# Banded attention chunks that hold a wide and a narrow head together, with a fourth query and key stack

## The chip, the cores and the metric

The kernel runs on one core of a Trainium2 chip. The metric is device time in microseconds (us) of one execution; several executions are timed and their median is given, and one more is profiled.

## The reference

One transformer layer, post-norm, on x of shape [2, 2048, 256]: attention with 16 heads of 16 columns and ALiBi bias, a residual and a layer norm, then a routed mixture of 7 experts with a no-op expert, a residual and a layer norm. The part that matters here is the attention:

```python
n_heads = 16; head_dim = 16
qkv = (x @ Wqkv + bqkv).reshape(B, L, 3, n_heads, head_dim)
scores = einsum('bqhd,bkhd->bhqk', q, k) / sqrt(head_dim)
scores = scores + slopes[None, :, None, None] * (-|i - j|)
probs = softmax(scores, axis=-1)
out = einsum('bhqk,bkhd->bqhd', probs, v).reshape(B, L, D)
x = layernorm(x + out @ Wout + bout)
```

The slope of head h is 2^(-h/2). Where slope times distance is beyond 104 the probability is zero, so head h needs only a band around the diagonal: 104 positions to each side for head 0, 1177 (rounded up to 16) for head 7, nearly everything from head 8 on.

## The kernel before, in words

The kernel has four stages on all engines: projections (to 113 us of the profiled execution), attention (to 785 us), output projection and routing, experts. Only attention is touched.

An **item** is one head of one batch: 32 of them. `ITEMS` lists them in pairs, a wide head (8 to 15) and then the narrow head with a number lower by 8. An item has 16 key blocks of 128 keys, and each key block has a **span** of query columns, the band around it (`spans`). `packed` lays the spans of all items one behind another into **chunks** of 1536 columns (three PSUM banks of 512): `CHAIN`, 489 chunks. A chunk holds pieces (item, key block, first and last query column, column in the chunk). As the items follow each other whole, a run of some 21 chunks of a wide head is followed by 5 to 20 chunks of the narrow one. In a wide chunk a piece is up to 1536 columns long, in a chunk of head 0 it is at most 336.

For each chunk c, in this order on the engines:

- **Scores**, TensorE, `score(c)`, the matmul of L987: for each piece, `score_cuts` splits the columns where the diagonal block begins or ends and at bank borders; each cut is 4 weight loads and 4 bf16 matmuls, one for each group of 32 array columns (32 keys each). They go to banks 0 to 2 or 3 to 5 by the parity of c. `score(c)` waits for the exponential of chunk c - 2 (`expd`), and in an item's first chunk for its loaded stack (`stack_in`).
- **Exponential**, ScalarE, one ACTIVATE of the whole chunk, L1031, from the banks into `prob`, a ring of 8 chunks in SBUF.
- **Diagonal blocks**, L1045: each key block's own 128 columns are multiplied with a table, even key blocks on VectorE and odd ones on GpSimd (heads 2 and 3 twice).
- **Values**, TensorE, `pv(c)`, L1011: `value_runs` splits each piece by query block j; block j goes to the column group j % 4, so each group keeps its own part of the output in PSUM bank 6 + n % 2. `value_turns` lines the runs of the four groups up in turns, the group with the most columns last. Each turn is one f32 matmul, two weight loads and two matmuls in the trace. `pv(c - 4)` stands behind `score(c)` on TensorE (`VALUE_LAG = 4`, `value_bursts`).
- **Division**, VectorE, in the slots of `divide_plan`: six slots after an item's last chunk the sums are copied out of PSUM (TAKE, L1053), and in one slot each follow SPREAD (L1059), four INVERT (a reciprocal of 128 columns, L1064) and SCALE (L1070). A slot also holds the diagonal blocks of the chunk of that number.

GpSimd copies an item's values into `v_head` (L1098) at the item's first chunk. SyncE's queue, in the order of the items, loads each item's query and key rows into one of three **stacks** (`STACKS = 3`, 11 DMAs of L259 to L293; item 0 is loaded earlier from ScalarE's queue), waiting for the last scores of the item three before, and stores the output of the item three before (L937).

## Time and profile before

| | |
|---|---|
| median of 3 runs | 1063.8 us (1063.44 to 1067.05) |
| profiled execution | 1064.59 us |
| its span, first to last instruction | 1062.8 us |
| TensorE busy | 1015.1 us, 96% |
| ScalarE busy | 811.9 us, 76% |
| VectorE busy | 453.5 us, 43% |
| GpSimd busy | 321.1 us, 30% |
| mean granted TensorE clock | 0.981 of 2.4 GHz |

The profiled execution lies 0.8 us above the median of the runs, and 1.8 us of it are outside the span. A busy share of TensorE is not its load at full rate: matmuls overlap, and their ends are modelled.

### The profile page before, as it was taken

The page shows a single profiled execution, that of the slowest core. Times are in us where ns is not written, and L with a number is a line of the kernel's source. Part 1 is how long each engine was busy: PE and PEld are TensorE (multiplying, and loading weights), DVE is VectorE, ACT ScalarE, POOL GpSimd, SP SyncE. Part 2 cuts the span into 40 slices and gives each one's busy share as a digit, 9 for nine tenths or more (in the row PEclk, how much of TensorE's full clock was granted, in tenths as well). Part 3 has the DMA queues.
Part 4 walks back from the last instruction along what each step waited for, and adds up shares of the span by engine and source line. Part 5 has one row for each costly group of instructions (what it writes and reads, how often), then busy time and mean ns, then how long its engine had stood idle before and what let it go on. Part 6 is the DMA issues. An engine that isn't in the chain of part 4 may idle for free. (4 is left out here: it accounts for less than half of the span.)

```text
span 1062.8 us, 40378 instructions
## 1 busy us (share of the span) xinstructions
PE 1015.1 (96%) x17922; PEld 720.6 (68%) x17922; DVE 453.5 (43%) x1064; ACT 811.9 (76%) x807; POOL 321.1 (30%) x486
## 2 busy tenths in 40 slices
PE   9999899999999999999999999999997399999997
PEld 6555576776676776877666776868686256666665
DVE  5778324564352432325355624323257611111165
ACT  3564799999999999999999999999966164211152
POOL 3333122234121121112232721211330255555433
PEclk9999999999999999999999999999999599999999
DMA  6755312212222111112332221120209246544473
GB/s 195 222 189 173 110 57 72 58 59 83 53 67 61 51 46 46 47 45 68 103 109 64 53 82 54 49 65 25 87 12 301 48 135 174 125 116 113 114 282 133
DMA packets 76562, 104.87 MB, mean 99 GB/s; under 512 B 13774, under 2 KB 62556, under 8 KB 76380
## 3 DMA queue, kind: packets, MB, share of 16 engines
q1 hardware_dynamic: 65852, 87.94, 26.6%
q0 software_dynamic: 6080, 9.06, 4.1%
q10 hardware_dynamic: 4448, 5.19, 1.5%
q8 instruction: 144, 2.36, 0.9%
q14 instruction: 38, 0.31, 0.1%
HBM read 66.49 MB, written 31.48 MB: 92 GB/s over the span
## 5 line engine op out<-in xcount | busy, mean ns | idle before, releaser
L1031 ACT ACTIVATE prob<-ps 128x1536 f32<-128x1536 f32 (+5 forms) x489 | 660.6, 1533 | 13.4 <-PE ps L987 12.1
L987 PE MATMUL ps<-q_stack,k_stack 111*32 111x512 bf16 (+25 forms) x9308 | 467.3, 302 | 7.0 <-issue 5.1
L1011 PE MATMUL ps<-prob,v_head 128*32 128x128 f32 (+6 forms) x7288 | 467.6, 338 | 2.5 <-issue 2.5
L987 PEld LDWEIGHTS ps<-q_stack,k_stack 111*32 111x32 bf16 (+2 forms) x9308 | 257.2, 96 | 132.2 <-ACT prob L1031 70.5
L1011 PEld LDWEIGHTS ps<-prob,v_head 128*32 128x32 f32 x7288 | 291.0, 110 | 53.4 <-issue 4.9
L1045 POOL TENSOR_TENSOR prob<-prob,near_bias 128x128 f32<-128x128 f32 x288 | 141.7, 496 | 500.6 <-ACT prob L1031 497.5
L1045 DVE TENSOR_TENSOR prob<-prob,near_bias 128x128 f32<-128x128 f32 x288 | 97.9, 348 | 400.4 <-ACT prob L1031 399.2
L1064 DVE RECIPROCAL o_rec<-o_den 128x128 f32<-128x128 f32 x128 | 113.8, 924 | 0.7
L1744 PE MATMUL ps<-xeT,w 128*128 128x512 f32 x224 | 99.2, 601 | 0.8 <-ACT xeT L1775 0.7
L1821 ACT ACTIVATE hT<-ps 128x512 f32<-128x512 f32 x28 | 16.7, 596 | 106.5 <-PE ps L1744 106.5
L1758 PE MATMUL ps<-w,hT 128*128 128x256 f32 x448 | 97.9, 379 | 0.0
L1758 PEld LDWEIGHTS ps<-w,hT 128*128 128x128 f32 x448 | 84.8, 190 | 11.5 <-issue 0.5
L1744 PEld LDWEIGHTS ps<-xeT,w 128*128 128x128 f32 x224 | 43.1, 193 | 52.9 <-issue 50.6
L502 PE MATMUL ps<-xT,w_qkv 128*128 128x512 f32 x128 | 60.1, 599 | 1.0 <-DVE w_qkv L740 1.0
L615 ACT ACTIVATE split<-ps,bias_qk_columns 128x512 bf16<-128x512 f32 x32 | 22.0, 687 | 44.3 <-PE ps L502 42.0
L1979 DVE TENSOR_SCALAR hT<-ps 128x512 f32<-128x512 f32 x28 | 19.4, 692 | 79.7 <-PE ps L1744 79.7
L863 POOL TENSOR_TENSOR square<-split 128x512 bf16<-128x512 bf16 x32 | 33.6, 1050 | 64.0 <-ACT split L615 63.9
L2032 POOL DMA_INDIRECT token_sums<-ye,slot_token x20 | 31.6, 1578 | 60.4 <-DVE ye L1995 42.3
L2012 POOL DMA_INDIRECT xe<-z_rows,slot_token x28 | 28.4, 1013 | 52.6 <-DVE slot_token L1582 44.4
L502 PEld LDWEIGHTS ps<-xT,w_qkv 128*128 128x128 f32 x128 | 23.6, 190 | 23.1 <-issue 19.4
L1995 DVE TENSOR_SCALAR ye<-ps,slot_weights 128x256 f32<-128x256 f32 x20 | 9.7, 484 | 65.5 <-PE ps L1758 65.5
L511 PEld LDWEIGHTS ps<-w_qkv,xT 128*128 128x128 f32 x128 | 24.1, 190 | 14.6 <-issue 10.5
(175 smaller groups left out, 610.7 us busy)
## 6 DMA issues: line engine op xcount, KB each, us to landing
qk_parts<-split SPq DMA_DIRECT2D x32, 384.0 KB, 3.0
w<-L_ffn_experts_inter_dram SPq DMA_DIRECT2D x7, 1024.0 KB, 6.4
w<-n_L_ffn_experts_out_dram SPq DMA_DIRECT2D x7, 1024.0 KB, 9.5
q_stack<-qk_parts SPq DMA_DIRECT2D x31, 192.0 KB
k_stack<-qk_parts SPq DMA_DIRECT2D x31, 192.0 KB
z_rows<-v SPq DMA_DIRECT2D x8, 516.0 KB, 8.8
heads<-o_out SPq DMA_DIRECT2D x128, 32.0 KB, 2.4
v<-in_L_attn_x_dram SPq DMA_DIRECT2D x8, 512.0 KB, 6.8
```

Source lines behind the costliest of these rows:

```text
L502: mm = pe.matmul(ps[:, 2 + m, :], w[:, k, m * P:(m + 1) * P], xT[n % 2][:, k, :], start=(k == 0), stop=(k == 1))
L511: mm = pe.matmul(ps[:, 6 + s % 2, 0:DX], xT[n % 2][:, k, s * P:(s + 1) * P], w[:, k, 2 * D:3 * D + EXTRA], start=(k == 0), stop=(k == 1))
L863: pool.tensor_tensor(square[m][:, :], split[m][:, 0, :], split[m][:, 0, :], ALU.mult)\
L987: mm = pe.matmul(ps[k:k + 32, SLOT_BANKS * (c % 2) + bank, col:col + z - a], k_st[n % STACKS][0:rows, kb * P + k:kb * P + k + 32], q_st[n ...
L1011: mm = pe.matmul(ps[32 * g:32 * g + 32, 6 + n % 2, column:column + width * times], vh[n % 2][:, kb, :], moving, start=(n, g) not in begun, ...
L1031: act.activation(prob[:, c % RING, 0:at + z - a], ps[:, bank:bank + SLOT_BANKS, :].rearrange("p c n -> p (c n)")[:, 0:at + z - a], ACT.Exp ...
L1045: eng.tensor_tensor(here, here, near[:, h, :], ALU.mult).then_inc(done, 1)
L1064: dve.reciprocal(o_rec[:, mine], o_den[:, mine]).then_inc(o_step, 1)
L1744: mm = pe.matmul(ps[:, 2 + j % 2, :], w1[par][:, k, j * P:(j + 1) * P], xeT[par][:, k, :], start=(k == 0), stop=(k == 1))
L1758: mm = pe.matmul(ps[:, 4 + s, 0:D], hT[:, j, s * P:(s + 1) * P], w2[par][:, j, :], start=(j == 0), stop=(j == FT - 1))
L2012: pool.indirect_dma_start(out=xe[e % 2][:, s, :], out_offset=None, in_=z_rows, in_offset=bass.IndirectOffsetOnAxis(ap=t["slot_token"][:, e ...
L2032: pool.indirect_dma_start(out=acc_rows, out_offset=bass.IndirectOffsetOnAxis(ap=t["slot_token"][:, e, s:s + 1], axis=0), in_=ye[e % 2][:, ...
```

## The change

- `packed` and `fill` give way to `mixed`: a pair of items (wide, narrow) is laid out together. The first 4 chunks of a pair hold the wide head alone; from then on each chunk begins with a share of the narrow head's columns (every second chunk a quarter more than the share) and is filled up with the wide head's. The share is sized so that the narrow head ends at least 3 chunks ahead of the wide one. Each pair begins a new chunk, so its last chunk may be short. `CHAIN` has 494 chunks.
- An item's chunks now overlap those of its partner, and the narrow item ends first. `ENDING` and `RANK` order the items by their last chunk for the division and the stores. `place_of` gives each item its output bank and values buffer, and `place_user_before` the item that must have ended before.
- There are four stacks. The fourth lies in the SBUF of `split`, a tile of the projections; item 3's load now waits for the stores from it (`parts_out`). Stores still follow the load of the item three on (`STORE_LAG = 3`).
- `part_shift` and `widen_shift` of the second batch (8 small VectorE instructions) move from the start of attention to slots 6, 7 and 8.
- `BIAS_AT` of the second batch goes by the chunk count. In the general branch, which these inputs don't take, a semaphore is replaced by others.

```diff
-STACKS = 3
+STACKS = 4
+STORE_LAG = 3
+NARROW_FROM, WIDE_LAST = 4, 3
+SHIFT_SLOT = 6
...
+def next_pieces(left, at, room):
+    pieces = []
+    while left and room > 0:
+        n, kb, a, end = left[0]
+        z = min(end, a + room)
+        if kb * P < z < kb * P + P:
+            z = kb * P
+        if z <= a:
+            break
+        pieces.append((n, kb, a, z, at))
+        at, room = at + z - a, room - (z - a)
+        left[0] = (n, kb, z, end)
+        if z == end:
+            left.pop(0)
+    return pieces, at
+
+def mixed(wide, narrow):
+    (n, h), (m, g) = wide, narrow
+    left = [[(item, kb, a, z) for kb, a, z in spans(head, 0)] for item, head in (wide, narrow)]
+    columns = [sum(z - a for *_, a, z in mine) for mine in left]
+    shared = -(-(sum(columns) - (NARROW_FROM + WIDE_LAST) * WIDTH) // WIDTH)
+    share = -(-columns[1] // shared // 16) * 16
+    chunks = []
+    while left[0] or left[1]:
+        pieces, at = [], 0
+        if len(chunks) >= NARROW_FROM and left[1]:
+            pieces, at = next_pieces(left[1], at, min(share + share // 4, WIDTH) if len(chunks) % 2 else share)
+        more, at = next_pieces(left[0], at, WIDTH - at)
+        if not left[0] and not more:
+            more, at = next_pieces(left[1], at, WIDTH - at)
+        chunks.append(pieces + more)
+    return chunks
...
-CHAIN = packed(ITEMS)
+CHAIN = [chunk for n in range(0, len(ITEMS), 2) for chunk in mixed((n, ITEMS[n][1]), (n + 1, ITEMS[n + 1][1]))]
...
+ENDING = sorted(range(len(ITEMS)), key=lambda n: LAST[n])
+RANK = [ENDING.index(n) for n in range(len(ITEMS))]
+
+def place_of(n):
+    return (n // 2 + n % 2) % 2
+
+def place_user_before(n):
+    earlier = [m for m in range(len(ITEMS)) if place_of(m) == place_of(n) and LAST[m] < FIRST[n]]
+    return max(earlier, key=lambda m: LAST[m]) if earlier else None
...
         if slot - VALUE_LAG - 2 in LAST:
-            n = LAST.index(slot - VALUE_LAG - 2)
+            n = RANK[LAST.index(slot - VALUE_LAG - 2)]
...
             if (b, h) == ITEMS[H]:
                 sp.wait_ge(t["shift_out"], 32)
+            if n == STACKS - 1:
                 for m in range(4):
                     sp.wait_ge(t["parts_out"][m], 16 * NCH)
...
-            if n >= STACKS:
-                store_turned_heads(n - STACKS)
+            if n >= STORE_LAG:
+                store_turned_heads(n - STORE_LAG)
...
-                    if n >= 2:
-                        pe.wait_ge(o_read, n - 1)
+                    if place_user_before(n) is not None:
+                        pe.wait_ge(o_read, RANK[place_user_before(n)] + 1)
...
-                mm = pe.matmul(ps[32 * g:32 * g + 32, 6 + n % 2, column:column + width * times],
-                               vh[n % 2][:, kb, :], moving, start=(n, g) not in begun, stop=False,
+                mm = pe.matmul(ps[32 * g:32 * g + 32, 6 + place_of(n), column:column + width * times],
+                               vh[place_of(n)][:, kb, :], moving, start=(n, g) not in begun, stop=False,
...
-        part_shift(dve, t, 1, 4)
-        for part in range(3):
-            widen_shift(dve, t, 1, part)
         for slot, steps in enumerate(DIVIDE):
+            if slot == SHIFT_SLOT:
+                part_shift(dve, t, 1, 4)
+            if 0 <= slot - SHIFT_SLOT < 3:
+                widen_shift(dve, t, 1, slot - SHIFT_SLOT)
...
+            split = v_life.enter_context(nc.sbuf_tensor("split", [P, 4, 3, CH], BF16))
+            t["split"] = [split[:, m, :, :] for m in range(4)]
+            spare = split[0:ROWS, :, :, :].rearrange("p m c n -> p (m c n)")
+            t["q_stack"].append(spare[:, 0:L])
+            t["k_stack"].append(spare[:, L:2 * L])
```

## Rows read from the trace of the kernel before

**Rows 1.** Costliest groups: busy, mean ns of one, then idle before and its releaser.

```profile
L1031 ACT ACTIVATE prob<-ps 128x1536 f32<-128x1536 f32 (+5 forms) x489 | 660.6, 1533 | 13.4 <-PE ps L987 12.1
...
L1011 PE MATMUL ps<-prob,v_head 128*32 128x128 f32 (+6 forms) x7288 | 467.6, 338 | 2.5 <-issue 2.5
```

**Rows 2.** Waits: total us, times, longest; the first three of attention.

```profile
PEld ps L987 <- ACT prob L1031: 70.5, 174, 1.4
...
PEld ps L987 <- issue: 14.5, 34, 1.7
...
ACT prob L1031 <- PE ps L987: 12.1, 16, 2.9
```

**Rows 3.** Timeline, ScalarE: start, us, calls, idle before; attention's exponentials.

```profile
114.17 5.48 ACT L1031 ACTIVATE prob<-ps 128x1536 f32<-128x1536 f32 x4 [2.89 <-PE ps L987]
119.88 1.45 ACT L1031 ACTIVATE prob<-ps 128x1536 f32<-128x1536 f32 x1 [0.23 <-PE ps L987]
122.16 23.09 ACT L1031 ACTIVATE prob<-ps 128x1536 f32<-128x1536 f32 x17 [0.82 <-PE ps L987]
...
785.29 1.28 ACT L1445 ACT_TABLE_LOAD   x1
```

**Rows 4.** Timeline, ScalarE, short windows: one wide stretch, then heads 4, 5 and 6.

```profile
405.05 20.28 ACT L1031 ACTIVATE prob<-ps 128x1536 f32<-128x1536 f32 x15
...
294.49 15.95 ACT L1031 ACTIVATE prob<-ps 128x1536 f32<-128x1536 f32 x11
...
336.96 8.74 ACT L1031 ACTIVATE prob<-ps 128x1536 f32<-128x1536 f32 x6
...
383.18 11.14 ACT L1031 ACTIVATE prob<-ps 128x1536 f32<-128x1536 f32 x8
```

**Rows 5.** Windows, busy us and instructions of each engine: one wide, then around heads 1 and 4.

```profile
282.00:293.00 11.00, 11.00 (x272) 6.92 (x268) 1.17 (x4) 11.00 (x9) 2.39 (x5) 1.00 0.17 45
...
176.30:194.20 17.90, 17.39 (x618) 14.76 (x610) 6.78 (x16) 17.14 (x14) 6.19 (x13) 1.00 0.24 79
...
296.20:307.60 11.40, 11.40 (x378) 10.98 (x372) 6.70 (x14) 11.18 (x8) 3.54 (x7) 1.00 0.12 45
```

**Rows 6.** Instruction queue (packets, MB, share), then TensorE's timeline in head 0's chunks.

```profile
q8 instruction: 144, 2.36, 0.9%
...
145.16 0.44 PE L987 MATMUL ps<-q_stack,k_stack 123*32 123x80 bf16 x21 [0.41 <-issue]
...
149.04 0.26 PE L987 MATMUL ps<-q_stack,k_stack 111*32 111x112 bf16 x4 [1.04 <-issue]
```

**Rows 7.** Start of attention: timeline of SyncE's queue and TensorE, windows, one store.

```profile
113.12 2.04 SPq L259 DMA_DIRECT2D q_stack<-qk_parts  x3
...
119.29 0.28 SPq L293 DMA_DIRECT2D q_stack<-shift_rows  x1
...
118.36 1.47 PE L987 MATMUL ps<-q_stack,k_stack 111*32 111x512 bf16 x12 [0.51 <-ACT prob L1031]
...
119.00:120.00 1.00, 1.00 (x12) 0.37 (x8) 0.00 (x0) 0.77 (x2) 0.00 (x0) 0.50 0.63 172
...
heads<-o_out SPq DMA_DIRECT2D x128, 32.0 KB, 2.4
```

**Rows 8.** End of attention: timeline of VectorE and TensorE.

```profile
787.40 0.69 DVE L1053 COPY o_sum<-ps 128x512 f32<-128x512 f32 x1 [1.97 <-PE ps L1011]
...
788.13 0.72 DVE L1059 STREAM_SHUFFLE o_den<-o_sum 128x512 f32<-128x512 f32 x1
788.89 3.39 DVE L1064 RECIPROCAL o_rec<-o_den 128x128 f32<-128x128 f32 x4
...
792.32 0.69 DVE L1070 TENSOR_TENSOR o_out<-o_sum,o_rec 128x512 f32<-128x512 f32 x1
...
792.49 7.85 PE L1419 MATMUL ps<-w_out,heads 128*128 128x265 f32 x34 [1.35 <-DVEq L1088]
```

More of the change, by code:

```diff
@@ L111, in filled @@
     return max((at + z - a for _, _, a, z, at in chunk), default=0)
-def packed(items):
-    chunks = [[]]
-    for n, (b, h) in enumerate(items):
-        at = filled(chunks[-1])
-        mine = next(new for new in (fill(n, h, at, more) for more in range(0, P, 16))
-                    if n + 1 == len(items) or filled(new[-1]) % P == 0)
-        chunks = chunks[:-1] + [chunks[-1] + mine[0]] + mine[1:]
-        if filled(chunks[-1]) == WIDTH:
-            chunks.append([])
-    return [chunk for chunk in chunks if chunk]
+def next_pieces(left, at, room):
[29 more added lines that the diff above has]
+    return chunks
 def own_column(piece):
@@ L181 @@
 FIRST, LAST = [uses[0] for uses in USES], [uses[-1] for uses in USES]
+ENDING = sorted(range(len(ITEMS)), key=lambda n: LAST[n])
[5 more added lines that the diff above has]
+    return max(earlier, key=lambda m: LAST[m]) if earlier else None
 def own_blocks(c, odd):
     return [(ITEMS[piece[0]][1], own_column(piece)) for piece in CHAIN[c] if own_column(piece) is not None and piece[1] % 2 == odd]
-BIAS_AT = [FIRST[-8] + 3 * c for c in range(QG)] + [FIRST[-1] + 3 * c for c in range(QG)]
+BIAS_AT = [FIRST[-8] + 3 * c for c in range(QG)] + [CHUNK_COUNT - 13 + 3 * c for c in range(QG)]
 def value_bursts():
@@ L964, in banded_sync @@
                 sp.sem_inc(t["heads_ready"], 1)
-        for n in range(len(ITEMS) - STACKS, len(ITEMS)):
+        for n in range(len(ITEMS) - STORE_LAG, len(ITEMS)):
             if n == len(ITEMS) - 2:
@@ L2136, in build @@
                 t[name] = v_life.enter_context(nc.sbuf_tensor(name, shape, F32))
-            t["q_stack"] = [v_life.enter_context(nc.sbuf_tensor(f"q_stack{k}", [ROWS, L], BF16)) for k in range(STACKS)]
-            t["k_stack"] = [v_life.enter_context(nc.sbuf_tensor(f"k_stack{k}", [ROWS, L], BF16)) for k in range(STACKS)]
+            t["q_stack"] = [v_life.enter_context(nc.sbuf_tensor(f"q_stack{k}", [ROWS, L], BF16)) for k in range(STACKS - 1)]
+            t["k_stack"] = [v_life.enter_context(nc.sbuf_tensor(f"k_stack{k}", [ROWS, L], BF16)) for k in range(STACKS - 1)]
             t["stack_in"] = [v_life.enter_context(nc.semaphore(f"stack_in{k}")) for k in range(STACKS)]
@@ L2142, in build @@
                 t[name] = v_life.enter_context(nc.sbuf_tensor(name, shape, dt))
-            t["split"] = [v_life.enter_context(nc.sbuf_tensor(f"split{m}", [P, 3, CH], BF16)) for m in range(4)]
+            split = v_life.enter_context(nc.sbuf_tensor("split", [P, 4, 3, CH], BF16))
[3 more added lines that the diff above has]
+            t["k_stack"].append(spare[:, L:2 * L])
             t["parts_out"] = [v_life.enter_context(nc.semaphore(f"parts_out{m}")) for m in range(4)]
```

29 lines of the change are left out of this document (14 added, 15 removed).

## The prediction

> **What bounds the kernel now.** I looked first for the engine that sets attention's pace, then at where that engine is late, then at what makes it late. The costliest groups name two candidates: ScalarE's 489 exponentials, 660.6 us busy, and TensorE's matmuls [rows 1]. The waits say how the two stand to each other: ScalarE waited 12.1 us in all for scores, 2.9 us of it ahead of its first call, and TensorE's score loads waited 70.5 us in 174 places for ScalarE [rows 2]. So ScalarE leads, and TensorE is close behind it. Attention runs from ScalarE's first exponential at 114.17 us to the table load that follows its last one at 785.29: 671.1 us [rows 3].
>
> The short windows of ScalarE's timeline give its price. A call's own record is about 1.45 us long and overlaps the next one, so n calls that end d us after the first began have a period of (d - 1.45) / (n - 1). In a wide stretch that is (20.28 - 1.45) / 14 = 1.345 us [rows 4]; that one call alone takes 1.45 is in [rows 3]. Columns make 748,256 / 1536 = 487.1 full calls, so at that period attention takes 655.2 us; 15.9 us of the 671.1 lie above it. About 9.2 us of these are the idle places of rows 2 without the first. The other 6.7 are calls that come a little late while no idle time is shown: in the narrow stretches of heads 4, 5 and 6 the periods are 1.450, 1.458 and 1.384 us [rows 4]. There TensorE sets the pace.
>
> Two properties of narrow chunks can be the reason, and both can be counted from the chunk lists that the code builds. First, **the deepest column group**. Values are split over four groups by query block. In a wide chunk each group has 384 of 1536 columns; in narrow chunks of heads 4 to 7 the deepest has 424 to 467 on average, and the next exponential needs the scores of all four. Second, **instructions**: a cut is 8 (loads and matmuls), a turn 4. A wide stretch issues 540 in 11 us, a narrow one 750 in 11.4 us, or 15.2 ns each, and around head 1 it is 1,228 in 17.9 us, or 14.6 ns each [rows 5]. In head 0's chunks, up to 160 instructions each, TensorE stops for 0.41 and 1.04 us with nothing that it waits for but "issue" [rows 6]. The instruction queue moved 144 packets of 16 KB [rows 6], which for TensorE's 35,844 instructions is one per 249: these stops look like instructions that haven't arrived. By the Trainium skill ("Runtime: NRT & Kernel Launch", Instruction fetch mechanics) blocks of 256 instructions are fetched ahead and the fetch is hidden, as dispatch is slower than the fill. The trace disagrees here, with the 1.04 us; were the page right, nothing below would change but the chance of the third rival.
>
> **The change part by part.**
>
> Exponentials. 494 calls of 747,584 columns are 486.7 full ones, 654.6 us at 1.345, and 7.3 more starts of a call. What a start costs is 1.345 less 1536 columns at the rate of the wide stretch; even at 0.07 us each it is +0.5 us. Sum 655.1, no gain.
>
> Work on TensorE. This is the term that decides. Cuts go from 2,327 to 2,724 and turns from 3,644 to 5,134, so the loads and matmuls of attention go from 33,192 to 42,328. The reason is that each share ends in the middle of spans, and that wide pieces are cut shorter. The deepest groups, summed over all chunks, go from 198,528 to 214,928 columns. The mixing takes the peaks down (from 160 to 124 instructions in a chunk's turn on TensorE) but it doesn't dilute the narrow chunks' property, it spreads it: 346 chunks are mixed, with 12.1 turns, 6.2 cuts, 95 instructions and a deepest group of 460 columns on average. Before, only 144 chunks belonged to a narrow head. Prices of a mixed chunk: at 14.6 and 15.2 ns an instruction [rows 5] it takes 1.39 and 1.45 us; the stretches of heads 4 to 6 had 8 to 13 turns and took 1.384 to 1.458 us [rows 4]; by the deepest group, head 4's 1.450 us at some 470 columns against 1.345 at 384 is 1.2 ns a column, which gives 1.43. The low bound is 1.345, ScalarE's own pace. I take 1.415, the middle of these rows: 346 x (1.415 - 1.345) = +24.2 us. The 148 unmixed chunks stay at ScalarE's pace; their room can't be lent, since scores run at most two chunks ahead. This replaces all of the 15.9 us but those at the start.
>
> Start. The sixth call began at 122.16, and its stretch has a period of (23.09 - 1.45) / 16 = 1.35, so the first six took 9.35 us, 1.3 us above the price; in that time the granted clock fell to 0.50, that is 1.2 GHz, for chunks 4 and 5 [rows 3, 7]. The narrow item is now needed at chunk 4, not at chunk 20. Its 11 loads leave SyncE's queue from 113.12 to 119.57 [rows 7], and a DMA of that queue lands 2.4 us later by the median of the small stores, so about 122.0. Chunk 4's scores began at 118.36 [rows 7]. `score(4)` stands ahead of every value matmul, so all of TensorE waits behind it, some 3.6 us; ScalarE has a chunk in hand and the slow clock had made chunk 5 late anyway, so I count +2.3 us on its path, between 0 and 3.6. Start in all 1.3 + 2.3 = 3.6.
>
> End. Before, the last item's sums were taken at 787.40, 2.1 us behind the last exponential, and 5.6 us later its output was scaled; TensorE's routing waited for that [rows 8]. Now the narrow item's last chunk is 487 of 493, so its SPREAD and reciprocals stand in slots 494 to 498, ahead of the wide item's TAKE in slot 499 on the same in-order engine: 0.72 + 3.39 us [rows 8] from shortly after the last exponential, and its SCALE of 0.69 behind. The TAKE comes about 2.3 us later than now and the end another 0.7: +3.0 us, between 0 (if the last values are late as well) and 4.8, the three together.
>
> At nothing: the shift instructions of the second batch move behind near blocks that VectorE reaches with four chunks in hand; the item 3 load waits for projections that ended before attention; the fourth stack lets loads go earlier, but the trace names only one stack wait, 0.3 us, so it buys nothing; the next pair's narrow item takes over the wide item's bank, whose TAKE stands in slot 30 for the first pair while the new values stand behind `score(33)`, 4 us later; if VectorE is late by more, that becomes a stall of the difference, pair by pair.
>
> **Sum.** 655.1 + 24.2 + 3.6 = 682.9 us of attention against 671.1, +11.8; with the end +14.8. From the profiled 1064.6 that is 1079.4, and as this execution lies 0.8 us above the median, 1079 us for the median.
>
> **The rivals.**
>
> 1. Faster: peaks are the whole cost. If TensorE is late only where a burst of small instructions exceeds what it has in hand, the mixed chunks, with peaks of 124 in place of 160, run at ScalarE's 1.345 us. The 24.2 us vanish: 1054.5, and without the losses at start and end 1049. For it: idle time of ScalarE is shown just in the narrow stretches [rows 2, 3]. Against it: heads 4 to 6 have no such bursts and still run at 1.38 to 1.46. It decides below 1.36 us per mixed chunk.
>
> 2. Hardly changed: groups even out from chunk to chunk. The deepest group changes from chunk to chunk, and over the mixed part of a pair the four sums of value columns differ by under 3%. If a group that is done goes on to the next scores while another is behind, only small costs per instruction stay. A mixed chunk at 1.37 us costs 8.7 in place of 24.2: 1063. By the Trainium skill ("TensorEngine Tiling (Array Packing)", Key Properties) the tiles operate independently, which is this rival's mechanism. Against it: head 4's stretch took 1.450 us though its four sums were within some 7%, which explains only a third of the 0.105.
>
> 3. Much slower: instruction supply. With 95 instructions in a chunk's turn the mixed part stands at the rate of the densest rows all the time, and a pair of head 0 or 1 has 101. At 15.2 ns and short of hand-overs, 1.46 us: +15.6 more, 1095. For it: the stops at "issue" [rows 2, 6]. It also needs that such stops come without a burst.
>
> 4. It doesn't do what it says: the mixture holds the chunks back by hand-over waits on banks or VectorE, as priced above. Some 1 us for each of 15 pairs on top of the forecast, 1094.
>
> **How the numbers follow.** Forecast 0.50 (mixed chunk at 1.385 to 1.44 us: 1069 to 1088). Rival 1: 0.14. Rival 2: 0.16. Rival 3: 0.16. Rival 4: 0.04. The range reaches from 1057, which takes in rival 2 and the edge of rival 1, to 1096. A change of 0.5%, 5.3 us, is about what a measurement of this kernel can tell from none: faster is below 1058.5, slower above 1069.1. Rival 1 is nearly all faster (0.13), rival 2 with the low edge of the forecast is the same (0.17), the rest is slower (0.70).
>
> **What would show it.** In the profile after, ScalarE's calls in the mixed stretches should have a period of about 1.415 us, and TensorE should be busy through with few waits for ScalarE: well under 70.5 us. The "issue" stops of head 0 should be gone or spread. ScalarE should sit idle for 2 to 4 us before its fifth call, behind a stack DMA. At the end, the o_sum copy should come 4 us or more behind the last exponential. A period of 1.345 in mixed chunks makes the prediction wrong, and so does a price that isn't TensorE's: an idle ScalarE with an idle TensorE beside it.

## The result, and the profile after

| | before | after |
|---|---|---|
| median | 1063.7 us (4 runs, 1063.4 to 1067.1) | 1128.0 us (4 runs, 1126.4 to 1129.8) |
| ratio to before | | 1.0597, 95% interval 1.057 to 1.0624 |
| profiled execution: time, span | 1064.6, 1062.8 us | 1128.5, 1126.8 us |
| first exponential to table load | 114.17 to 785.29, 671.1 us | 113.86 to 843.39, 729.5 us |
| loads and matmuls of attention in the code | 33,192 | 42,328 |

The change makes the kernel 6% slower, 64 us where I forecast 15, and outside the range. Attention takes 58.4 us more. What follows it takes 5.9 more: 3.2 of these are the end term below, the other 2.7 were not followed up. The page after shows ScalarE's exponentials, TensorE's matmuls and the queue that brings instructions; the columns are those of [rows 1, 6].

```profile
L1073 ACT ACTIVATE prob<-ps 128x1536 f32<-128x1536 f32 (+6 forms) x494 | 676.7, 1441 | 55.7 <-PE ps L1029 50.1
L1053 PE MATMUL ps<-prob,v_head 128*32 128x128 f32 (+13 forms) x10268 | 520.2, 289 | 5.4 <-issue 5.2
...
q8 instruction: 180, 2.95, 1.1%
```

The waits after (total us, times, longest), for comparison with [rows 2]:

```profile
ACT prob L1073 <- PE ps L1029: 50.1, 56, 10.4
...
PEld ps L1029 <- issue: 24.1, 52, 1.7
...
PEld ps L1029 <- DMA q_stack<-shift_rows: 16.7, 3, 11.0
PEld ps L1029 <- ACT prob L1073: 16.4, 43, 1.4
...
PE ps L1029 <- issue: 10.0, 15, 1.5
...
PEld ps L1029 <- DMA split<-shift_rows: 3.6, 3, 1.9
```

The leader has changed. TensorE's score loads waited 70.5 us for ScalarE before and 16.4 now; ScalarE waited 12.1 us for scores before and 50.1 now. And two releasers have grown or are new: "issue" and the DMAs of the stacks. Only 50.1 of the 74 us that attention stands above its 655.1 us of exponentials are shown as ScalarE's idle time; the rest is again calls that come a little late.

ScalarE's timeline after: the start, a long stretch of mixed chunks, the place of one later stack (item 21), and the end:

```profile
113.86 5.48 ACT L1073 ACTIVATE prob<-ps 128x1536 f32<-128x1536 f32 x4 [2.89 <-PE ps L1029]
129.75 1.45 ACT L1073 ACTIVATE prob<-ps 128x1536 f32<-128x1536 f32 x1 [10.40 <-PE ps L1029]
132.31 1.45 ACT L1073 ACTIVATE prob<-ps 128x1536 f32<-128x1536 f32 x1 [1.11 <-PE ps L1029]
134.96 14.64 ACT L1073 ACTIVATE prob<-ps 128x1536 f32<-128x1536 f32 x10 [1.20 <-PE ps L1029]
...
327.15 87.82 ACT L1073 ACTIVATE prob<-ps 128x1536 f32<-128x1536 f32 x63 [0.75 <-PE ps L1029]
...
566.20 1.45 ACT L1073 ACTIVATE prob<-ps 128x1536 f32<-128x1536 f32 x1 [4.05 <-PE ps L1029]
...
843.39 1.28 ACT L1488 ACT_TABLE_LOAD   x1
```

The first six calls take 134.96 - 113.86 = 21.1 us; before it was 9.35. The stretch at 327.15 has a period of (87.82 - 1.45) / 62 = 1.393 us.

### The profile page after: what moved, and what is told of

The parts are those of the page before. It is cut to its first block, busy times and chain, and to the rows that moved or that the text cites. A ratio compares the mean times of both kernels' runs of the same rounds, so it can differ in the third digit from the quotient of the medians.

```text
span 1126.8 us, 49529 instructions
## 1 busy us (share of the span) xinstructions
PE 1049.9 (93%) x22490; PEld 837.8 (74%) x22490; DVE 443.7 (39%) x1064; ACT 828.0 (73%) x812; POOL 323.4 (29%) x486
## 4 chain that ended last, share of the span: by engine, by line
PE 72%; DMA 7%; SPq 4%; issue 3%; DVE 2%; ACT 2%; POOL 0%; POOLq 0%; ACTq 0%; DVEq 0%
PE ps L1029 26%; PE ps L1053 25%; PE ps L1801 9%; PE ps L1787 8%; DMA split<-shift_rows 3%; DMA q_stack<-shift_rows 3%; PE ps L1462 2%; SPq L317 1%; SPq L301 1%; ACT prob L1073 1%; PE ps L1775 1%; PE ps L1481 1%; SPq L319 0%; DMA xe<-z_rows,slot_token 0%; DVE o_rec L1106 0%
## 5 line engine op out<-in xcount | busy, mean ns | idle before, releaser
L1073 ACT ACTIVATE prob<-ps 128x1536 f32<-128x1536 f32 (+6 forms) x494 | 676.7, 1441 | 55.7 <-PE ps L1029 50.1
L1053 PE MATMUL ps<-prob,v_head 128*32 128x128 f32 (+13 forms) x10268 | 520.2, 289 | 5.4 <-issue 5.2
L1029 PE MATMUL ps<-q_stack,k_stack 111*32 111x512 bf16 (+40 forms) x8624 | 459.6, 288 | 24.2 <-DMA q_stack<-shift_rows 15.0
L1053 PEld LDWEIGHTS ps<-prob,v_head 128*32 128x32 f32 x10268 | 383.7, 110 | 39.5 <-issue 10.4
L1029 PEld LDWEIGHTS ps<-q_stack,k_stack 123*32 123x32 bf16 (+1 forms) x8624 | 288.4, 96 | 64.9 <-issue 16.9
L1087 DVE TENSOR_TENSOR prob<-prob,near_bias 128x128 f32<-128x128 f32 x288 | 90.0, 319 | 475.6 <-ACT prob L1073 474.4
L1029 PE MATMUL ps<-split 111*32 111x512 bf16 (+39 forms) x2272 | 125.8, 260 | 5.4 <-issue 2.8
L1029 PEld LDWEIGHTS ps<-split 111*32 111x32 bf16 (+2 forms) x2272 | 81.5, 96 | 22.7 <-issue 7.2
L1864 ACT ACTIVATE hT<-ps 128x512 f32<-128x512 f32 x28 | 16.7, 596 | 107.0 <-PE ps L1787 107.0
```

The costliest lines, as they stand in the source:

```text
L1029: mm = pe.matmul(ps[k:k + 32, SLOT_BANKS * (c % 2) + bank, col:col + z - a], k_st[n % STACKS][0:rows, kb * P + k:kb * P + k + 32], q_st[n ...
L1053: mm = pe.matmul(ps[32 * g:32 * g + 32, 6 + place_of(n), column:column + width * times], vh[place_of(n)][:, kb, :], moving, start=(n, g) n ...
L1073: act.activation(prob[:, c % RING, 0:at + z - a], ps[:, bank:bank + SLOT_BANKS, :].rearrange("p c n -> p (c n)")[:, 0:at + z - a], ACT.Exp ...
L1087: eng.tensor_tensor(here, here, near[:, h, :], ALU.mult).then_inc(done, 1)
```

## The experiments

Each ratio is to the kernel before on the same chip, whose median lay between 1063.7 and 1070.4 us; "before" stands for it. A difference between two kernels is taken from their ratios where they ran on different chips. The kernels whose names begin with b_, and a_half, a_whole and a_aligned, were timed once. Single times of the kernel before lie up to 7.5 us apart on one chip, so a difference of a few us between two of these is not told from none.

**Instructions alone.** Two kernels leave the old chunk list and end the wide heads' score cuts more often. Nothing else changes: no column, no wait, no chunk.

```
+    if ITEMS[piece[0]][1] >= H // 2:
+        ends |= {a - at + m * 256 for m in range(1, WIDTH // 256) if a < a - at + m * 256 < z}
```

> The kernel before, with the scores of its wide heads cut at every 256 columns of the chunk as well: 39,896 loads and matmuls in attention in place of 33,192, 76 in a wide chunk in place of 56; columns, deepest groups (198,528) and chunks are the same. Theory A (TensorE can be fed one instruction per 14.6 to 15.2 ns, and nothing else of an instruction costs time): 76 x 15.2 = 1.16 us fits under ScalarE's 1.345, so no change, 1064 +- 3 us. Theory B (each cut adds a fixed cost of its own to every column group, some 10 ns, whatever the supply): 838 more cuts and TensorE within 0.04 us of ScalarE in wide chunks, +5 to +12 us. Theory C (deepest group alone): no change.

1078.2 us against 1064.5, +14, with 39,896 loads and matmuls, 76 in a wide chunk. Theory A, which said no change, missed this.

> The same with cuts at every 192 columns: 51,264 loads and matmuls, 110 in a wide chunk, more than the 95 of a mixed chunk of the changed kernel; the columns of the deepest group stay at 387 in a wide chunk. Theory A (supply): a wide chunk takes 110 x 14.6 to 15.2 ns = 1.60 to 1.67 us in place of 1.345, x 323 = +82 to +105 us, about 1150 to 1170 us. Theory B (10 ns a cut in each group): 2,259 more cuts, +15 to +23 us. Theory C (deepest group): no change, 1064 us.

With 192 in place of 256 it is 1194.9 us, +130, with 51,264 loads and matmuls, 110 in a wide chunk. Its waits, as in [rows 2]:

```profile
ACT prob L1033 <- PE ps L989: 120.6, 146, 4.0
PEld ps L989 <- issue: 107.2, 174, 2.6
...
PE ps L989 <- issue: 73.7, 98, 2.4
```

Its instruction queue on the page:

```profile
q8 instruction: 215, 3.52, 1.2%
```

A window in its wide stretch (columns as in [rows 5]), and one stop there in TensorE's timeline:

```profile
400.00:430.00 30.00, 25.85 (x983) 21.06 (x975) 7.57 (x15) 25.24 (x19) 3.57 (x8) 1.00 0.15 44
```

```profile
405.61 0.43 PE L989 MATMUL ps<-q_stack,k_stack 111*32 111x64 bf16 x15 [1.49 <-issue]
```

In 30 us TensorE issues 983 + 975 instructions, 15.3 ns each, and is busy for only 25.85 us: it stands still with work at hand, in a chunk that has the columns of a cheap one. The queue moves one packet for 250 of TensorE's instructions here too (53,916 / 215).

The trace also shows what the stops are. Number TensorE's loads and matmuls in the order of their starts: all 101 stops of matmuls at "issue" that are longer than 0.3 us stand at the same place in every 256 (193 or 194 of them go before), each 1.2 to 1.6 us after the end of a 16 KB packet of the instruction queue. The same holds for each such stop in attention in the kernel before (8) and the kernel after (19). These packets follow each other every 3.8 us in b_cut192 (the median), 14.8 ns for each of 256 instructions, and in attention they stand no closer than 3.2 us in any trace of this case. So TensorE waits there for its next block of instructions.

So the number of instructions has a price, by itself, from about 85 to 90 in a chunk's turn on (1.345 us / 15.3 ns = 88), and its sign in the trace is a matmul's stop at "issue". 110 in a chunk cost 0.40 us in each of 323 wide chunks. 76 cost 0.04: that is an average of chunks with 48 to 132, and 54 of the 323 lie over 88. The count over three chunks in a row that is used further down gives 13.6 us more than before for b_cut256 and 141.7 for b_cut192, where +14 and +130 were measured. Rival 3's mechanism is real.

**Depth of the column groups.** Three kernels take one block of 128 value columns of each wide chunk and compute it separately: b_split in its own group, b_rotate in the next group, which is another one in each chunk, and b_fixed always in group 1 in place of group 0. The cut shows b_rotate; b_split has `turn % GROUPS` for both, b_fixed has 0 and 1.

```
+    if all(ITEMS[piece[0]][1] >= H // 2 for piece in chunk):
+        turn = CHAIN.index(chunk)
+        source, target = turn % GROUPS, (turn + 1) % GROUPS
+        long = [m for m, run in enumerate(queues[source]) if run[5] > 1]
...
```

> Control for the next two: the kernel before, where in each wide chunk one value matmul of 256 or 384 columns is split, its last 128 columns as a turn of their own in the same column group. 34,484 loads and matmuls in place of 33,192, 60 in a wide chunk; each group still has 384 columns. Every theory: within 4 us of 1064.

1070.3 us against 1069.2: +1.

> As b_split, but the 128 columns go to the next column group (those sums land in the wrong group, so part of the value sums is misplaced): the deepest group of a wide chunk has 512 columns in place of 384, another has 256, and which group is deep changes with each chunk; instructions and columns are those of b_split. Theory C (each chunk waits for its deepest group): 323 wide chunks at 640 + 853 = 1.49 us in place of 1.345, +47 us over b_split. Rival (groups even out from chunk to chunk): as b_split, within 5 us. Supply alone (theory A): as b_split.

1074.2 us, +4 on b_split.

> As b_rotate, but always from the first to the second group, so the second group has 512 value columns in every wide chunk and nothing can even out. Every theory that knows columns at all: 640 + 853 = 1.49 us in each of 323 wide chunks, +45 us or somewhat more over b_split. It shows what a full imbalance costs, as a measure for b_rotate.

1127.2 us, +57 on b_split. The deepest group has 512 columns in both; what differs is whether it is always the same one. 57 / 323 = 0.18 us a chunk where it is; where it moves on it is 0.01, which single runs do not tell from nothing. The windows of b_fixed and b_rotate in the wide stretch show TensorE busy all the time in both:

```profile
405.00:425.00 20.00, 20.00 (x504) 17.11 (x496) 7.42 (x15) 19.75 (x16) 4.02 (x8) 1.00 0.21 58
```

```profile
405.00:425.00 20.00, 20.00 (x466) 15.83 (x458) 7.00 (x13) 20.00 (x16) 2.82 (x7) 1.00 0.12 37
```

So groups do even out from chunk to chunk, as rival 2 says, and my price "by the deepest group" of a chunk was no price. By the Trainium skill ("TensorEngine Tiling (Array Packing)", Key Properties) tiles operate independently; by that rule b_rotate's +4 agrees.

**Values at half size, in the kernel after (a_half).** Each value matmul reads half of its columns; loads and matmuls keep their number.

```
-                    moving = slab[:, at:at + width]
+                    moving = slab[:, at:at + width // 2]
...
```

> The changed kernel with every value matmul streaming half of its columns (half of the value sums are left out, VectorE adds 1 to what it takes so that the division stays finite, and clears the two banks once): the same 42,328 loads and matmuls, but the deepest group of a mixed chunk falls from 460 to 230 columns, so the columns of a mixed chunk take 640 + 383 ns. Theory A (supply): the period of a mixed chunk stays, 1.40 to 1.48 us, and the time stays within 15 us of the changed kernel's 1128. Theory C (deepest group): TensorE falls under ScalarE's pace, mixed chunks run at 1.345, 346 x 0.13 = 45 us less, about 1083 us, of which the start still costs 10.

1114.9 us, 13 less than the kernel after, still 50 above before. Its waits:

```profile
PEld ps L1029 <- ACT prob L1073: 88.7, 301, 1.4
ACT prob L1073 <- PE ps L1029: 57.4, 58, 10.5
PEld ps L1029 <- issue: 38.8, 67, 1.7
```

Half of the value columns gone buys a fifth of the loss. TensorE now waits for ScalarE in 301 places, and ScalarE for TensorE no less than in the kernel after (57.4 against 50.1): it has slack in many places and is late in others all the same. This understates what the columns are worth, as the loads wait longer for stacks here (30.1 us against 20.3), and 41 us of attention run at a granted clock of 0.50, against 17 in the kernel after. How much more than 13 us the columns are worth with these taken off was not measured. What stands is that the waits for "issue" grow with fewer columns and the same instructions.

**The start.** In a_early the second item's stack is loaded together with the first one's, during the projections.

```
+                    load_shift_rows(sp, t, shift_dram, ITEMS[1][1], 0, 1)
...
+                    load_q_piece(act, t, parts_dram, q_pos, ITEMS[1][1], b, 1, ROW_POS, piece)
```

> The changed kernel with the stack of item 1, the first narrow head, loaded in the projections beside that of item 0 (each of ScalarE's ten stack DMAs issued twice, and one more of SyncE's). If the 10.4 us idle of ScalarE before its fifth call and the half clock after it come from that load alone, 10 to 12 us less: 1116 to 1118 us. If the second and third item's loads or the clock hold chunk 4 to 7 anyway, less than 5 us. The ten DMAs more on ScalarE's queue in the projections could give back up to 3 us.

1124.7 us, ratio 1.0561 (1.0511 to 1.061): 3 or 4 us better, which the two intervals don't tell from none. ScalarE's timeline says why:

```profile
108.21 0.69 ACT L658 ACTIVATE split<-ps,bias_qk_columns 128x512 bf16<-128x512 f32 x1 [6.66 <-DMA qk_parts<-split]
...
126.77 15.30 ACT L1076 ACTIVATE prob<-ps 128x1536 f32<-128x1536 f32 x11 [4.94 <-PE ps L1032]
```

The stop of 10.4 us is gone, 11 calls follow each other, but attention begins 12.9 us later, since the projections now wait for stores. The stall was moved. One number does better. In a_start the first pair's narrow head begins at chunk 10.

```
+    first = 10 if n == 0 else NARROW_FROM
...
-        if len(chunks) >= NARROW_FROM and left[1]:
+        if len(chunks) >= first and left[1]:
```

> The kernel after with one number changed: the first pair's narrow head starts at chunk 10 in place of chunk 4; all other pairs as they are. My theory of the start (the second item's stack lands some 9 us after chunk 4 wants it, and the half clock then drags on) makes this 8 to 12 us faster than the kernel after, about 1117 us. If the loss at the start is the dense chunks there, which are only moved, the time stays within 3 us of 1128.

1118.4 us, ratio 1.051 (1.049 to 1.053): 0.87% of 1064, 9 us, come back.

**Order of stores and stacks (a_store).** SyncE issues the stores of two items one after the other, behind the loads of the next pair, in place of one store behind each stack.

```
-            if n >= STORE_LAG:
-                store_turned_heads(n - STORE_LAG)
+            if n >= STORE_LAG + 2 and n % 2:
+                store_turned_heads(n - 5)
+                store_turned_heads(n - 4)
...
```

> The changed kernel with SyncE's queue in another order: the loads of both items of a pair first, then the stores of the two items that ended before, so that a load isn't held behind a store that waits for VectorE (418 us of such waits in the trace of the changed kernel). If late stacks cost what TensorE waits for them in that trace after the start, 4 to 6 us less than the changed kernel: 1122 to 1124 us, and no wait for a stack but the first. If the loads are late because they take long to land, no change.

1111.6 us, ratio 1.0429 (1.0394 to 1.0465): 1.7%, 18 us less than the kernel after, and attention takes 711.0 in place of 729.5 us. Of the stack waits only the first is left:

```profile
PEld ps L1030 <- DMA q_stack<-shift_rows: 10.5, 1, 10.5
```

The gain is more than the waits for stacks that are gone (16.7 + 3.6 - 10.5 = 9.8 us), and three times the 4 to 6 us expected. Laid side by side by ScalarE's calls, the two traces differ by 11.4 us in the four pairs in which TensorE waited for a later stack (7.5 of them in the pair of items 20 and 21), and by 7 us in the others, where the trace shows no such wait of note. The clock isn't the reason for these: both have 17 us of attention at 0.50. They were not isolated; the kernel after and a_start, whose chunks differ only in the first pair, lie 3 us apart over the other pairs.

**Whole column groups (a_whole).** Scores as one 128-wide matmul in place of four 32-wide ones.

```
-                    for k in range(0, P, 32):
+                    for k in range(0, P, P):
...
```

> The changed kernel with each cut of the scores as one matmul of 128 array columns in place of four of 32: the same columns, chunks and values, but 2,724 x 6 = 16,344 loads and matmuls fewer (25,984 in place of 42,328; about 58 in a mixed chunk). Theory A (supply): mixed chunks are no longer short of instructions; what is left is ScalarE's pace, the start (+12) and the deepest group: 346 x 0.1 = 35 us less than 1128, about 1090, and the issue waits of TensorE fall from 50 to under 5 us. Against it: between a 128-wide score matmul and a 32-wide value matmul the array may have to run empty, twice a chunk; at 0.1 us each that is 494 x 0.2 = +99 us, which would hide the gain (1190). Then the waits at issue still have to vanish, and the idle time of TensorE shows between scores and values.

1232.1 us against 1069.2, 99 more than the kernel after by the ratios, with 16,344 fewer loads and matmuls. In its timeline scores and values no longer overlap:

```profile
399.78 0.42 PE L1053 MATMUL ps<-prob,v_head 128*32 128x256 f32 x7
400.13 0.83 PE L1029 MATMUL ps<-q_stack,k_stack 123*128 123x512 bf16 x4
400.89 1.11 PE L1053 MATMUL ps<-prob,v_head 128*32 128x128 f32 x24
```

This kernel says nothing against the instructions' price: it swaps it for another, some 0.2 us a chunk (99 / 494). Its matmuls no longer stop at "issue" at all in attention, as expected. Its score loads wait 106.6 us for "issue" all the same, in 363 places: on a load that word alone is no sign of missing instructions.

**Fewer instructions in a mixed chunk.** First the shares are made multiples of 128 columns, so that they seldom end inside a block (a_aligned), then the narrow head is given a large share in every second chunk (a_alt), and a_alt with the first narrow head at chunk 10 and the last one ended 9 chunks early (a_best).

```
-    share = -(-columns[1] // shared // 16) * 16
+    share = -(-columns[1] // shared // P) * P
...
```

> The changed kernel with the narrow head's share rounded up to whole blocks of 128 columns and equal in every mixed chunk (no quarter more in every second one): the wide head's pieces then begin and end at block borders. Everything else of the mixture stays; 39,480 loads and matmuls in place of 42,328, peaks of 112 in place of 124, but deepest groups of 220,800 columns in place of 214,928. Theory A, supply at 15.5 ns an instruction taken over any three chunks in a row: that sum lies 49.5 us above ScalarE's pace in the changed kernel, 17.3 in the kernel before and 17.7 here, so 1128 - 32 = 1096 us. Theory C (deepest group): 5,872 columns more at 1.2 ns, +7, 1135 us. A price of mixing as such (hand-overs, overlapping items): no change, 1128.

1131.5 us, against 1070.4 for before: no gain, where 32 us were forecast.

```
+    both = -(-columns[1] // (shared // 2) // P) * P
+    large = min(both, WIDTH)
...
+        if len(chunks) >= first and left[1] and (large, both - large)[(len(chunks) - first) % 2]:
```

> As a_aligned, but the narrow head's columns stand in every second mixed chunk, twice as many (in heads 6 and 7, which don't fit, the rest stands in the chunk between): 36,568 loads and matmuls. Theory A, the same sum over three chunks: 11.7 us above ScalarE's pace, so 1128 - 38 = 1090 us, of which start and end still cost 15. With these taken off it would be level with the kernel before or a little under it. A price of mixing as such: well above 1100.

1131.4 us, ratio 1.0585 (1.0552 to 1.0617). Its waits:

```profile
PEld ps L1031 <- DMA q_stack<-shift_rows: 25.7, 5, 11.2
PEld ps L1031 <- issue: 23.8, 68, 1.7
...
PEld ps L1031 <- DMA split<-shift_rows: 14.6, 3, 5.2
```

> a_alt, with the first pair's narrow head beginning at chunk 10 in place of 4, when its stack has landed, and the last pair's ending 10 chunks ahead of the last, so that its division isn't ahead of the last item's. 36,676 loads and matmuls, 12.2 us above ScalarE's pace by the sum over three chunks. If the start costs what the changed kernel's trace shows (about 11 us) and the end 3: 1090 - 14 = 1076 us. If the supply sum is right to 5 us it is within 10 us of the kernel before, 1066; faster than it only if the hand-overs cost nothing.

1118.4 us, ratio 1.0463 (1.043 to 1.0495). The three are misses of mine: I had made the chunks lighter, and what came to the front was the stacks, 36.5 us of waits in a_aligned and 40.3 in a_alt against 20.3 in the kernel after. With the stops came the clock: both run 41 us of attention at 0.50, the kernel after 17. No kernel has these chunks with the other order of the queue, so what they are worth without the stops is not shown. This sent me to the order of stores and stacks above. With that order, and a share pattern for each pair that was chosen by counting instructions over any three chunks in a row, the next kernel still overlaps the two heads, in 33,288 loads and matmuls (in the expectations from a_alt on, these counts are 80 too low):

```
+LAYOUTS = ((3, 4, 3), (3, 7, 3), (1, 8, 3), (3, 5, 3), (3, 4, 5), (3, 9, 3), (1, 13, 8), (1, 13, 8))
+FIRST_LAYOUT, LAST_LAYOUT = (3, 9, 3), (1, 12, 9)
...
+    period, first, last = FIRST_LAYOUT if n == 0 else LAST_LAYOUT if n == len(ITEMS) - 2 else LAYOUTS[n // 2 % 8]
...
+    shares = [min(WIDTH, max(0, whole - turn * WIDTH)) for turn in range(period)]
```

> The changed kernel with a_store's queue order and a layout by table: per pair a period (the narrow head's columns stand in every first, or first and second, of 1, 2 or 3 chunks, in whole blocks), its first and last chunk; the first pair's narrow head begins at chunk 9 and the last pair's ends 9 ahead. 494 chunks, 33,208 loads and matmuls in place of 42,328 (before: 33,192), two heads in nearly the same 346 chunks less the empty ones. Theory A (supply at 15.5 ns over three chunks): 2.6 us above ScalarE's pace in place of 49.5, so with the start at +1 to +3 and no late stacks 655 + 3 + 3 = 661 us of attention: 1056 +- 5 us, faster than the kernel before by up to 1%. If mixing itself (two items in flight, shorter pieces, hand-overs) is what costs: above 1080.

1069.7 us, ratio 1.0029 (1.001 to 1.0048): some 60 of the 64 us are gone. It is still some 10 us above what I expected (1056, 1% ahead of before). In the trace attention takes 670.9 us, not 661: the first ten calls come 3.9 us late, and the short last chunk of each pair costs more than its columns, see below. One long stretch of the middle pairs runs at ScalarE's price:

```profile
305.26 146.72 ACT L1080 ACTIVATE prob<-ps 128x1536 f32<-128x1536 f32 x109 [0.54 <-PE ps L1036]
```

Its last call is a short one of 0.72 us, so the period is (146.72 - 0.72) / 108 = 1.352 us. The kernel before takes 1.352 us over the calls of the same numbers. Having two items in flight, with their banks, buffers and divisions, costs nothing here. But a_tuned mixes far less inside a chunk than the kernel after: by its chunk list 94 chunks hold both heads (11 of the 109 in this stretch) and 98 the narrow one alone, where the kernel after has 346 with both. That 346 such chunks would cost nothing at a low count of instructions is not shown. Then the decisive one: the same chunks, with the score cuts of the wide heads ended every 256 columns by the two lines of b_cut256, 40,992 loads and matmuls.

> The kernel a_tuned (mixed chunks whose narrow spans are kept whole, 33,208 loads and matmuls of attention) with the score cuts of the wide heads ended every 256 columns: the same columns, the same chunks, the same waits, but 40,912 instructions, close to the 42,328 of the kernel after. If instructions are the price of the mixed chunk, the count over three chunks in a row at 15.5 ns forecasts +26 us on a_tuned's 1069.7, about 1096. If what a_tuned mended was the place of the narrow columns and not the number of instructions, it stays within 5 us of 1070.

1086.8 us, ratio 1.0205 (1.018 to 1.023): +1.76% on a_tuned, 19 us. That is three quarters of the 26 forecast, in chunks that differ from a_tuned's by instructions alone. The matmuls of scores and values stop at "issue" for 7.6 us in a_pad, 1.5 in a_tuned, 7.6 in the kernel before and 15.2 in the kernel after; the rest of the price is calls that come a little late.

**A version slightly ahead of both.** a_tuned had two rests in its timeline: ScalarE's idle time at the first narrow chunk, and the last sums, taken 4.3 us behind the last exponential. a_final begins the first narrow head at chunk 10 and ends the last one 14 chunks early; a_later begins at chunk 13.

```
-FIRST_LAYOUT, LAST_LAYOUT = (3, 9, 3), (1, 12, 9)
+FIRST_LAYOUT, LAST_LAYOUT = (3, 10, 3), (1, 6, 14)
```

> a_tuned with the first pair's narrow head from chunk 10 and the last pair's ended 14 chunks before the last one, so that its division no longer stands ahead of the wide head's. Instruction supply is unchanged. I expect the 2.0 us idle at the start and the 2.6 us at the end to go: 1065 to 1067 us, 0 to 3 us below the kernel before of the same chip. If the end's delay is not the queue on VectorE, it stays at 1069 to 1070.

1062.5 us, ratio 0.998 (0.9969 to 0.9992). The end is mended (the sums are taken at 787.51, 1.64 us behind the table load at 785.87); the start is not, as one 3.47 us stop is left, in which TensorE waits for the stack until 130.02:

```profile
130.02 1.47 PE L1036 MATMUL ps<-q_stack,k_stack 99*32 99x128 bf16 x60 [2.97 <-DMA q_stack<-shift_rows]
```

> a_final with the first narrow head from chunk 13 in place of chunk 10. In a_final ScalarE still sat idle for 3.47 and 0.90 us around 131 us, because the second item's stack landed at about 130 us and chunk 10 wanted it 3 us earlier. If that landing time does not depend on the chunk list, chunk 13 wants it after it is there: the wait goes, and the time falls by 2 to 4 us to about 1059 to 1060, 4 us below the kernel before. If the landing moves with the demand, the wait stays and so does the time, 1062 to 1063.

1066.2 us against 1070.1, ratio 0.9965 (0.9946 to 0.9983): 3.7 us ahead of the kernel before, and 3.7 us is what its attention is shorter (114.72 to 782.10, 667.4 us). No wait for a stack is left, and the first stretch is unbroken:

```profile
114.72 25.63 ACT L1080 ACTIVATE prob<-ps 128x1536 f32<-128x1536 f32 x19 [2.89 <-PE ps L1036]
```

The stack is there at 128 to 130 us in the kernel after and a_final, which want it at different times, and in time for a_later.

## Why the prediction was wrong

The direction held, the mechanism (work on TensorE, in instructions) held in part, and four terms were too small. In the profiled execution attention takes 729.5 us where the sum said 682.9. The start and the short chunks are read from the trace, the stacks' term is the difference to another kernel, and the mixed chunks' part is what remains, so it takes up the errors of the others:

| term | forecast | measured | how |
|---|---|---|---|
| exponentials, by columns | 654.6 | 654.6 | 1.345 us for 1536 columns, as before |
| more starts of calls (short last chunks) | 0.5 | 5.3 | 15 of them: worth 7.9 by columns, saved 2.6 |
| start above the price | 3.6 | 13.0 | 21.1 for six calls less 6 x 1.345 |
| late stacks (the queue's order) | 0 | 18.5 | 729.5 less a_store's 711.0 |
| mixed chunks above the price | 24.2 | 38.1 | the rest: 0.110 us x 346 |
| end | +3.0 | +3.2 | table load to warm activation: 10.96 us, before 7.77 |

**The mixed chunk, +13.9 us missed.** I took 1.415 us, the middle of rows of narrow stretches; the remainder says 1.455, the upper end of the rows that I had at hand, and rival 3 had said 1.46. The step that failed is the choice among prices. (Its 95 instructions are off as well: 6.2 cuts and 12.1 turns make 98, or 94 in a turn on TensorE, where the values of an earlier chunk stand.) Of the three I listed, by instructions (1.39 to 1.45), by stretches (1.384 to 1.458) and by the deepest group (1.43), the last one is refuted by b_rotate, and the first has a threshold that an average hides: some 95 instructions are an average of heavy pairs and light ones, and what lies under some 88 in one pair isn't given back to another. A count over any three chunks in a row at 15.5 ns each, above 1.345 us, gives 17.3 us for before (where 15.9 lay above the price), 49.5 for after, 28.8 for a_pad and 2.6 for a_tuned. The measured step is smaller than the count's from a_tuned to a_pad, 19 in place of 26, and for the kernel after, some 38 in place of 49.5. It fails for a_aligned and a_alt, whose stack waits it doesn't see.

The weight I gave to rival 3 was too small, 0.16, because it needed "that such stops come without a burst". b_cut192 shows that they do. The Trainium skill ("Runtime: NRT & Kernel Launch", Instruction fetch mechanics), by which the fetch of instructions is hidden, is contradicted by b_cut192: its score matmuls stop for 73.7 us at "issue", the long stops at one place in every 256 instructions and shortly behind an instruction packet, and it takes 130 us more. (The 107.2 us of its score loads are not to be added: the two engines' waits overlap.)

**The short last chunks, +4.8 us missed.** Each pair begins a new chunk, so its last one is short, and I counted it by its columns and 0.07 us for the start of the call. In the kernel after, the one with the fewest has 256:

```profile
326.03 0.38 ACT L1073 ACTIVATE prob<-ps 128x256 f32<-128x256 f32 x1
```

Its own call takes 0.38 us, but the next begins only at 327.15, 1.12 us after this one began, and TensorE's scores end the wait. They may begin only when the call before the short one has left its banks, so a short call buys little. It is a price of beginning each pair anew, and the later versions with `mixed` pay it too.

**The start, +9.4 us missed.** The place was right and the landing wrong. SyncE's queue, after:

```profile
118.71 0.28 SPq L335 DMA_DIRECT2D q_stack<-shift_rows  x1
119.03 1.89 SPq L301 DMA_DIRECT2D q_stack<-qk_parts  x3
```

TensorE's timeline there, and a window of the time that follows:

```profile
128.22 1.47 PE L1029 MATMUL ps<-q_stack,k_stack 99*32 99x128 bf16 x24 [10.68 <-DMA q_stack<-shift_rows]
```

```profile
121.00:134.00 13.00, 5.78 (x100) 3.24 (x104) 0.51 (x3) 2.90 (x2) 0.73 (x2) 0.50 0.31 101
```

The last load of the stack is issued by 118.99 and TensorE gets it at 128.2, 9.2 us later, where I took 2.4 from a 32 KB store of the same queue [rows 7]. A landing time of a small store is no row for a stack of eleven loads with two more stacks right behind it. The last line shows the second part, which the prediction had not counted: TensorE stood still for 10.7 us and its granted clock fell to 0.50, that is 1.2 GHz, and stayed there until about 134; the next calls came 1.1 and 1.2 us late. a_start gives back 9 us. The hint was in the trace of before: its own loads of this stack were wanted only at chunk 20.

**Late stacks, 18.5 us, counted at nothing.** The step that failed is "the trace names only one stack wait, 0.3 us, so it buys nothing". The order of the queue is worth 18 us by a_store; 7.5 of them lie in the pair of the stop below, and some 7 in pairs without such a wait. That a resource isn't waited for in the trace of before says nothing of it where the change makes each item live longer: a stack is in use from its pair's chunk 4 to the end, its load is allowed only when an earlier item has ended, and SyncE issues it behind a store that waits for a division. SyncE's waits for VectorE's outputs from 100 to 850 us (total us, times, longest), then item 21's load, after:

```profile
SPq L978 <- DVE o_out L1112: 416.4, 17, 39.0
...
540.80 2.75 SPq L978 DMA_DIRECT2D heads<-o_out  x4
543.60 0.59 SPq L949 DMA_DIRECT2D v<-in_L_attn_x_dram  x1
544.24 3.18 SPq L301 DMA_DIRECT2D q_stack<-qk_parts  x3
...
551.39 0.28 SPq L335 DMA_DIRECT2D q_stack<-shift_rows  x1
```

It stands behind the store and a row of x, is issued by 551.67, and is there at about 564.5. Rival 4, which put 15 us on hand-over waits in all pairs, named banks and VectorE, not this. Its size was near, its place was not; I had given it 0.04.

**The end, right.** The last o_sum copy comes at 847.72, 4.3 us behind the table load, before 2.1: "4 us or more" held. The narrow head's reciprocals stand ahead of it:

```profile
844.41 3.39 DVE L1106 RECIPROCAL o_rec<-o_den 128x128 f32<-128x128 f32 x4
847.72 0.63 DVE L1095 COPY o_sum<-ps 128x512 f32<-128x512 f32 x1
```

**Of the signs that I named**, TensorE's waits for ScalarE fell as said (16.4 us, "well under 70.5"), the stops at "issue" did not go or spread thin but grew from 14.5 to 24.1 us (of the score loads), and ScalarE idled before its fifth call behind a stack, 10.4 us and not 2 to 4. Rival 1 is wrong for this change, and still has a true core: a_tuned, which takes the averages down and not only the peaks, does run a long stretch at 1.352 us.

**Open.** How the 38.1 us divide between the number of instructions and other properties of the mixed chunk was not measured in the kernel after itself. From a_tuned (1.0029) to a_pad (1.0205) 19 us are instructions. From a_pad to the kernel after without the losses of start and stacks (1.0597 - 0.0168 - 0.0087 = 1.0342) another 15 us lie in 1,300 more instructions that stand closer together (the count over three chunks gives 20.7 for them), or in something else, such as the 346 chunks that hold both heads against 94.

## What to carry to other kernels

A rearrangement that evens out columns can multiply small instructions; count the instructions that the in-order engine issues in each turn of the leading engine, over a few turns in a row, and treat the highest sustained rate in the trace as a wall and not as a point on a slope. For every buffer whose first use moves earlier or whose life becomes longer, follow its load from the release through the queue to the landing, with the landing taken from a load of the same size; that nobody waits for it in the trace before says nothing. Don't count a short chunk by its columns where the next chunk's inputs can't come earlier. A stop of the matrix engine also costs what the lower clock takes behind it.

## What the runs showed of the hardware

- TensorE issues short bursts faster than it can go on. Before, 57 matmuls and about as many loads go through in 1.04 us, 9 ns each, and a stop at "issue" of 1.04 us begins 0.9 us later; over 30 us it was 15.3 ns each in b_cut192. The long stops stand at one place in every 256 instructions, 1.2 to 1.6 us behind a packet of the instruction queue.

```profile
146.09 1.04 PE L987 MATMUL ps<-q_stack,k_stack 111*32 111x112 bf16 x57
```

- Four 32-wide column groups run on independently past the end of a chunk: 128 columns more in a group that stays the same cost 0.18 us a chunk, in a group that changes no more than single runs tell from nothing (0.01).
- A matmul over all 128 columns of the array between 32-wide ones ends that overlap: some 0.2 us a chunk in a_whole, although it takes 39% of the instructions away.
- Eleven loads of a stack took 9 to 13 us from the last issue to the landing, while a 32 KB store of the same queue takes 2.6.
